# Attention sums loaded by head and multiplied by stored reciprocals, in the second stage of a two-layer graph network kernel

## What is computed

```python
# layer 0: masked attention with 8 heads of 16, then a feed-forward block
qkv = layer_norm(x, g1, be1) @ w_qkv
scores = einsum('nhd,mhd->hnm', q, k) * 16 ** -0.5      # masked by adj
out = einsum('hnm,mhd->nhd', softmax(scores), v).reshape(n, 128)
x = x + out @ w_proj + b_proj
ff = gelu(layer_norm(x, g2, be2) @ w1 + b1) @ w2 + b2
x = x + ff
# layer 1: attention whose score belongs to the row alone, projection, residual, layer norm
```

## Time and profile before

| | us |
|---|---|
| median of 3 runs | 1278.1 |
| lowest and highest run | 1275.76, 1278.79 |
| the profiled execution, its own time | 1278.86 |
| its span from first to last instruction | 1276.8 |
| PE busy | 1178.1 (92%) |
| DVE busy | 1138.7 (89%) |
| ACT busy | 1052.6 (82%) |
| POOL busy | 982.9 (77%) |

### The profile page before, as it was taken

How to read it: one execution, slowest core, us unless ns; L and a number is a source line. 1 busy time by engine, 2 the same in 40 slices (tenths; PEclk the granted TensorE clock), 3 DMA queues, 4 the chain that set the end, 5 groups by cost and what they waited for, 6 DMA issues and landing times. The chain is left out here.

```text
span 1276.8 us, 31455 instructions
## 1 busy us (share of the span) xinstructions
PE 1178.1 (92%) x11639; PEld 332.7 (26%) x11639; DVE 1138.7 (89%) x1616; ACT 1052.6 (82%) x1194; POOL 982.9 (77%) x1028
## 2 busy tenths in 40 slices
PE   5888889999999999999999899999999998999976
PEld 2222222111111111111111111111111126775433
DVE  5989889999999999999999899999999994656756
ACT  4978889999999999999999899999999992441000
POOL 5867768999999989999998788888888872544222
PEclk8989899999999999999999999999999998999988
DMA  4332324754554455555445545555455457405870
GB/s 175 91 117 75 84 87 129 209 157 134 165 151 134 133 167 160 155 150 162 138 133 163 147 143 158 154 153 145 133 167 149 134 154 292 180 20 236 328 301 28
DMA packets 52672, 194.40 MB, mean 152 GB/s; under 512 B 6497, under 2 KB 20641, under 8 KB 42273
## 3 DMA queue, kind: packets, MB, share of 16 engines
q1 hardware_dynamic: 38944, 156.65, 34.5%
q0 software_dynamic: 9216, 33.56, 12.9%
q10 hardware_dynamic: 4352, 2.10, 0.6%
HBM read 114.69 MB, written 44.04 MB: 124 GB/s over the span
## 5 line engine op out<-in xcount | busy, mean ns | idle before, releaser
L1394 DVE SCALAR_TENSOR_TENSOR probs<-m,ps 128x512 f32<-128x512 bf16 (+1 forms) x1024 | 926.6, 950 | 30.9 <-PE ps L1586 14.8
L1291 ACT ACTIVATE probs<-probs 128x1536 f32<-128x1536 f32 x512 | 848.5, 1658 | 0.9
L1188 POOL TENSOR_TENSOR probs<-probs,m 128x512 f32<-128x512 f32 x512 | 634.7, 1270 | 118.9 <-ACT probs L1285 107.9
L1601 PE MATMUL ps<-probs,v_sb 128*17 128x512 f32 x4096 | 543.5, 603 | 0.0
L1586 PE MATMUL ps<-kq 32*128 32x512 bf16 x6144 | 429.3, 382 | 61.6 <-DVE probs L1394 33.8
L1285 ACT ACTIVATE probs<-ps 128x512 f32<-128x512 f32 x512 | 392.1, 766 | 33.3 <-PE ps L1586 32.1
L1586 PEld LDWEIGHTS ps<-kq 32*128 32x128 bf16 x6144 | 117.0, 93 | 580.0 <-ACT probs L1285 429.8
L1181 POOL TENSOR_SCALAR m<-adj_in 128x512 bf16<-128x512 int32 x256 | 192.9, 754 | 0.2
L1601 PEld LDWEIGHTS ps<-probs,v_sb 128*17 128x17 f32 x4096 | 68.2, 95 | 219.8 <-issue 208.3
L453 ACT ACTIVATE probs<-ps 128x512 f32<-128x512 f32 x8 | 4.8, 597 | 86.1 <-PE ps L798 84.1
L376 POOL TENSOR_TENSOR v_sb<-v_sb,cols 128x4 f32<-128x4 f32 (+1 forms) x9 | 8.8, 975 | 74.3 <-DVE v_sb L649 74.3
(11 more groups left out here) (140 smaller groups left out, 652.0 us busy)
## 6 DMA issues: line engine op xcount, KB each, us to landing
adj_in<-in_adj_t SPq DMA_DIRECT2D x64, 1024.0 KB, 5.7
mask_t<-m SPq DMA_DIRECT2D x64, 512.0 KB, 2.9
counts<-m POOLq DMA_DIRECT2D x64, 512.0 KB, 4.6
kq<-mask_t SPq DMA_DIRECT2D x16, 2048.0 KB, 9.7
counts_t<-counts SPq DMA_DIRECT2D x8, 512.0 KB, 7.4
attn_t<-acc_sb SPq DMA_DIRECT2D x16, 256.0 KB, 6.7
adj_in<-attn_t SPq DMA_DIRECT2D x8, 512.0 KB, 3.9
v_sb<-counts_t SPq DMA_DIRECT2D x8, 512.0 KB, 7.0
```

What stands on the lines that cost most here:

```text
L1188: nc.gpsimd.tensor_tensor(pr, pr, m01[:, (k // 2) % MRING, :], ALU.mult).then_inc(postmasked, 1)
L1291: nc.scalar.activation(pr, pr, ACT.Exp, scale=UNIT).then_inc(exped, 1)
L1394: nc.vector.scalar_tensor_tensor(out=pr, in0=m.to_broadcast([P, n, CH]), scalar=1.0, in1=ps[:, b:b + n, :], op0=ALU.subtract, op1=ALU.add)\
L1601: last = nc.tensor.matmul(ps[RT * hh:RT * hh + VW, 6 + g, :], v_sb[:, t, h * VW:(h + 1) * VW], probs[:, k % SLOTS, hh // 2, (hh % 2) * CH: ...
```

## The change

Layout and order of the block stage change; what is computed stays.

- `load_sums` no longer loads the stored sums as they lie. It fetches only the 16 rows of each head, packed, so that row 16·head + d holds dimension d of that head: two transfers of 64 rows of 2 KB for the tile's first half, `outs[..][:, 0, :]`. A third one fetches the reciprocals from a new DRAM tensor `inverse_t`, each head's row of 512 repeated 16 times, into `outs[..][:, 1, :]`. With x these are four transfers a chunk in place of two.
- The reciprocals are made one chunk at a time during the attention: SP fetches the 17th rows of the chunk just stored in eight transfers (`load_head_sums`, 16x32 each) into a 128x32 tile, DVE inverts it (`invert`, called in `masks` at step 24 of the next chunk), SP stores it (`store_inverse`). For the last chunk SP does so in the block stage, with DVE's `invert` at `i == 0`.
- `normalise_att` is one 128x512 multiplication from SBUF to `attT`. `turn_acc`, `turn_att` and `turned_att` are gone, with PSUM banks 3 to 5 used by `turn_h2` alone.
- `project(i+1)` stands ahead of `ff1(i)`; `project(0)` between the third last and second last `products` of the attention.
- `x1` has two tiles, so `first_sum(c)` waits for the readers of chunk c-2.

The core of the diff:

```diff
         def load_sums(sp, c):
             if c >= 2:
-                sp.wait_ge(acc_turned, c - 1)
+                sp.wait_ge(attT_made, c - 1)
                 sp.wait_ge(xb_made, c - 1)
-            sp.dma_start(acc[c % 2][:, :, :], a_dram[c, :, :, :]).then_inc(acc_in[c % 2], 16)
+            for g in range(2):
+                rows_of = a_dram[c, :, g, :].rearrange("(h r) n -> h r n", r=RT)
+                sp.dma_start(outs[c % 2][g * HG * HD:(g + 1) * HG * HD, 0, :], rows_of[:, 0:HD, :])\
+                    .then_inc(acc_in[c % 2], 16)
+            sp.dma_start(outs[c % 2][:, 1, :], inv_dram[c].rearrange("h (a n) -> h a n", a=1).to_broadcast([H, HD, CH]))\
+                .then_inc(acc_in[c % 2], 16)
...
+        def load_head_sums(sp, c):
+            sp.wait_ge(acc_stored, 32 * (c + 1))
+            if c > 0:
+                sp.wait_ge(inverse_stored, 16 * c)
+            for g in range(2):
+                rows_of = a_dram[c % NC, :, g, :].rearrange("(h r) (s n) -> h r s n", r=RT, s=HD)
+                for hh in range(HG):
+                    at = (g * HG + hh) * HD
+                    sp.dma_start(head_sums[at:at + HD, :], rows_of[hh, HD, :, :]).then_inc(sums_in, 16)
+
+        def store_inverse(sp, c):
+            sp.wait_ge(inverted, c + 1)
+            sp.dma_start(inv_dram[c % NC].rearrange("h (s n) -> (h s) n", s=HD), head_sums[:, :])\
+                .then_inc(inverse_stored, 16)
+
+        def invert(dve, c):
+            dve.wait_ge(sums_in, 16 * H * (c + 1))
+            nc.vector.reciprocal(head_sums[:, :], head_sums[:, :]).then_inc(inverted, 1)
...
             load_sums(sp, 2)
             load_edges(sp, 1)
+            load_head_sums(sp, NC * R - 1)
             for n in range(2, ERING):
                 load_sums(sp, n + 1)
                 load_edges(sp, n)
+            store_inverse(sp, NC * R - 1)
...
             def normalise_att(c):
...
+                dve.wait_ge(acc_in[c % 2], LOADED * (c // 2 + 1))
                 if c >= 1:
...
+                    dve.wait_ge(projected, c)
+                nc.vector.tensor_tensor(attT, outs[c % 2][:, 0, :], outs[c % 2][:, 1, :], ALU.mult)\
+                    .then_inc(attT_made, 1)
...
             products(TLS * R - 4)
-            turn_acc(0)
             products(TLS * R - 3)
+            project(0)
             products(TLS * R - 2)
-            turn_att(0)
             products(TLS * R - 1)
-            project(0)
...
-            turn_acc(1)
             turn_h2(0)
             for i in range(NC):
-                ff1(i, (0, 1))
-                if i + 1 < NC:
-                    turn_att(i + 1)
-                ff1(i, (2, 3))
                 if i + 1 < NC:
                     project(i + 1)
+                ff1(i, (0, 1, 2, 3))
                 if i >= 1:
                     turn_x2(i - 1)
                 ff2(i)
-                if i + 2 < NC:
-                    turn_acc(i + 2)
...
+                if G >= per_chunk and G % per_chunk == 2:
+                    load_head_sums(sp, G // per_chunk - 1)
+                if G >= per_chunk and G % per_chunk == 4:
+                    store_inverse(sp, G // per_chunk - 1)
...
             def masks(k, begin):
+                if k >= begin + 2 * NT and k % (2 * NT) == 24:
+                    invert(dve, k // (2 * NT) - 1)
```

More of the change, by code:

```diff
@@ L383, in tail_scalar @@
             nc.scalar.activation(small[:, 7, 0:1], cols[:, 9:10], ACT.Gelu_apprx_tanh).then_inc(warmed, 1)
-            def turned_att(c):
-                act.wait_ge(att_turned, c + 1)
-                if c >= 1:
-                    act.wait_ge(projected, c)
-                nc.scalar.activation(attT, ps[:, B_TURN, :], ACT.Copy).then_inc(attT_made, 1)
             def turned_h2(c):
@@ L503, in first_sum @@
                 dve.wait_ge(xb_made, c + 1)
[L504 to L507 removed]
+                if c >= 2:
+                    dve.wait_ge(x1b_made, c - 1)
+                    dve.wait_ge(h2_made, c - 1)
+                nc.vector.tensor_tensor(x1[c % 2], by_tile(proj_bank(c)), xb[c % 2], ALU.add).then_inc(x1_made, 1)
                 dve.wait_ge(x1_made, c + 1)
                 for s in range(SUB):
[L510 removed]
+                    last = nc.vector.bn_stats(bn2[:, s, :], x1[c % 2][:, s, :])
                 last.then_inc(bn2_made, 1)
@@ L525, in normalise_x1 @@
                 for s in range(SUB):
-                    last = nc.vector.tensor_scalar(h2[:, s, :], x1[:, s, :], mv2[:, s, 0:1],
+                    last = nc.vector.tensor_scalar(h2[:, s, :], x1[c % 2][:, s, :], mv2[:, s, 0:1],
                                                    rstd2[:, s:s + 1], ALU.subtract, ALU.mult)
@@ L576, in tail_vector @@
                     normalise_att(i + 2)
+                if i == 0:
+                    invert(dve, NC * R - 1)
                 if i >= 1:
@@ L682, in tail_tensor @@
             pe.wait_ge(tail_in, N_TAIL_IN)
-            def turn_acc(c):
-                pe.wait_ge(acc_in[c % 2], 32 * (c // 2) + 32)
-                if c >= 1:
-                    pe.wait_ge(att_made, c)
-                else:
-                    pe.wait_ge(opened, TLS * R)
-                    pe.wait_ge(premasked, 2 * TLS * R)
-                for g in range(2):
-                    for s in range(SUB):
-                        last = nc.tensor.transpose(ps[:, B_ACC + g, s * P:(s + 1) * P],
-                                                   acc[c % 2][:, g, s * P:(s + 1) * P], identf[:, :])
-                last.then_inc(acc_turned, 1)
-            def turn_att(c):
-                pe.wait_ge(att_made, c + 1)
-                if c >= 1:
-                    pe.wait_ge(h2T_made, c)
-                for s in range(SUB):
-                    last = nc.tensor.transpose(ps[:, B_TURN, s * P:(s + 1) * P],
-                                               att[:, s * H:(s + 1) * H, :].rearrange("p h d -> p (h d)"),
-                                               identf[:, :])
-                last.then_inc(att_turned, 1)
             def project(c):
@@ L710, in project @@
                     pe.wait_ge(x1_made, c)
+                else:
+                    pe.wait_ge(opened, TLS * R)
+                    pe.wait_ge(premasked, 2 * TLS * R)
                 if c == 1:
@@ L1068, in second @@
                 store_acc(NC - 1)
-                sp.wait_ge(acc_stored, 32 * NC)
+                load_head_sums(sp, NC - 1)
+                store_inverse(sp, NC - 1)
+                sp.wait_ge(inverse_stored, 16 * NC)
                 sp.wait_ge(tail_in, N_TAIL_IN)
@@ L1085, in second @@
                         store_acc(G // per_chunk - 1)
+                    if G >= GROUPS + per_chunk and G % per_chunk == 2:
+                        load_head_sums(sp, G // per_chunk - 1)
+                    if G >= GROUPS + per_chunk and G % per_chunk == 4:
+                        store_inverse(sp, G // per_chunk - 1)
             def tail(sp, R):
@@ L1469, in second @@
                     copy_acc(NC - 1, g)
+                invert(dve, NC - 1)
                 all_reach(dve, phase)
```

49 lines of the change are left out of this document (14 added, 35 removed).

## The result

**Slower: 1283.61 us in the median of 5 executions (1281.56 to 1283.73), against 1276.79 (1275.40 to 1278.79) for the kernel before beside it, ratio 1.0049 [1.0035, 1.0063].** In a second measurement (`e0_changed` below) the ratio was 1.0038 [1.0022, 1.0054]. Forecast was 1274.6 in a range up to 1281.5. The profiled execution took 1281.56 us with a span of 1279.6, to be read against 1278.86 and 1276.8 before. That profile of before lies 2 to 3.5 us over the medians of its later runs (1275.4 to 1276.8), so differences of spans are good to about 3 us; differences inside one stage are sharper. The two profiled executions are 2.70 us apart, the medians 6.82: the profile of before is above all five of its runs, that of after is the shortest of its five.

The account below looks back on a forecast made before the run. PE was taken to bound the block stage, a DVE chain just under it. Attention +0.1, start and turn 0 0, turns -0.5, -1.9, -1.2 sum to -3.5: 1278.86 to 1275.4, 1274.6 on the median, range 1269.5 to 1281.5.

Parts of the forecast that it names:

- Start: Start of the block stage: `first_sum(0)` some 0.3 us earlier, PE at half clock, `ff1(0)` at 1062.8, 0.5 later.
- last paragraph: Signs for right or wrong; a load of sums landing after its multiplication could start would be something not counted.
- Turns: Block stage: turn 1 10.7 us, turns 2 to 5 10.75, turn 6 9.9; gains 0.5, 1.9 and 1.2 us.
- second chain: Block stage turn: `first_sum` through normalisation to `turn_h2`, 4.52 us, lies just under PE's bound; some tenths idle before `turn_h2`.
- Turn 0: First turn of the block stage: `ff1(1)` at 1075.15 against 1075.16 before, balance with the start 0.
- Attention: Seven added reciprocals on DVE cost 0.1 us in all, bounds nothing and 2.5; small transfers taken as nothing.
- Rival (c): Attention: POOL holds the reciprocals, 1.2 us each over seven, 8.4 in all, giving 1283.0, slower; chance 0.15.
- Rival (b): Block stage: the multiplication comes behind POOL's L335, waits 1.2 us, turn about 11.2, total 1277.6; chance 0.18.
- Rival (a): Block stage: PE alone bounds the turn, 9.91 us in turns 2 to 5, 3.4 more won, 1271.2; chance 0.17.
- Second x1 tile: Block stage: gives nothing, since the wait of `first_sum` ended with PE, not POOL.
- ACT's copy: ACT loses the copy L389; no gain, since it was not the bound.
- last stage: The stage after the block stage shifts whole, with no change of its own.

Follow-up runs that it names:

- e0_changed: The changed kernel measured once more, nothing altered: 1281.34 us, 1.0038 of the kernel before.
- e11: The kernel before, with only its load of sums replaced by the three transfers of the changed kernel (wrong data): 1285.12 us, 1.0053 of the kernel before.
- e4: The changed kernel with each chunk's sums and factors loaded in one transfer of 128 rows of 4 KB (wrong data): 1272.11 us, 0.9967 of the kernel before.
- e12: The changed kernel with the same rows picked and repeated in another order, 16 as outermost count, five transfers a load set: 1272.90 us, 0.9976 of the kernel before.
- e3: The changed kernel with picks kept, but reciprocals loaded from 128 distinct rows instead of repeated ones (wrong factors): 1274.58 us, 0.9966 of the kernel before.
- e6: The changed kernel with reciprocals still repeated, but sums loaded as 128 rows as they lie, without picking: 1272.37 us, 0.9977 of the kernel before.
- e9: The changed kernel with loads packed DRAM to DRAM during the attention, and `hidden_low` moved behind the normalisation: 1272.99 us, 0.9964 of the kernel before.
- e1: The changed kernel with `project(0)` moved behind the last two products: 1279.40 us, 1.0036 of the kernel before.
- e5: The changed kernel with `project(0)` behind the last two products and, on POOL, `root(0)` and `x1_bias(0)` ahead of `input_bias(1)`: 1280.12 us, 1.0027 of the kernel before.
- e13: The changed kernel with 16-outermost loads, `project(0)` behind the last products, `root(0)` and `x1_bias(0)` ahead of `input_bias(1)`: 1270.89 us, 0.9970 of the kernel before.
- e7: The changed kernel with picks and repeats made DRAM to DRAM during the attention, then one plain 512 KB load: 1270.93 us, 0.9948 of the kernel before.

## Why the prediction was wrong

**The step that failed: the loads of sums were not costed.** The step *Start* says "`normalise_att(0)` and `project(0)` leave the way of the last products earlier, so `first_sum(0)` starts right behind the second copy, some 0.3 before 1055.81". It took the new transfers to land like those of before (1050.1 and 1052.2), though the working names the other new DMAs and what each may delay. They landed at 1053.0 and 1061.4, and the start was 5.16 late, 6.16 counted from the end of the attention. The same omission made the turns from 1078.49 and 1101.35 last 12.08 and 13.30, 1.30 and 2.52 above 10.78: 3.8 of the 4.0 by which turns 1 to 5 missed; in the first of these two turns 0.73 of the 1.30 is the multiplication meeting POOL, which it does only because it is late. `e11` puts this on the loads alone, `e4` and `e12` take it away and leave the forecast's side: 0.9967 and 0.9976, where 1274.6 to 1278.1 was 0.9973. That agreement is closer than its parts (see the sum below) and in part luck. The last paragraph named "a load of sums landing after its multiplication could start" as something not counted. It was named and left without a price.

In the transfers the cause is the outermost count. Measured: counts of 4 and 8 give 228 GB/s, a count of 16 on the same rows 388. The Trainium skill ("DMA: Bandwidth & Descriptors", sections "Why a DMA increments its semaphore by 16 and not by 1" and "Rules for kernel authors") says that the slowest dimension of more than one element sets how many of the 16 engines a transfer runs on, and that for hardware-driven queues they are the lowest-numbered ones. The trace agrees with the number: 4 and 8 late steps for the transfers with counts of 4 and 8, and a DMA share of 0.24 to 0.25 at 90 to 99 GB/s while the last 4 steps of a mask load are outstanding. By that rule picks would lie on engines 0 to 3 and repeats on 0 to 7, on top of each other. The records do not number the engines, but that every mask load waits for just 4 late steps fits it.

One link is not shown: why the other engines slowed down too. The mean share stayed at 1.00 while the rate halved, so packets took longer in general. Those of 16 KB (the mask load's) that started from 1052 to 1056 took 0.61 us in the median before and in `e12`, 1.09 in the changed kernel and 1.10 in `e3`, but 0.62 in `e6`. So it comes with the picks, and its cause is open; the order in which `e12` reads the rows may have a part in it.

**Turns: right in size, partly wrong in reason.** Forecast 10.75, measured 10.78; last 9.9, measured 9.71. Timeline of PE over one turn of the changed kernel:

```profile
1125.43 3.79 PE L731 MATMUL ps<-q_shift,tail_words 128*128 128x512 f32 x8
1129.06 0.60 PE L723 MATMUL ps<-identf,probs 128*128 128x128 f32 x4
1130.00 3.84 PE L740 MATMUL ps<-tail_words,probs 128*128 128x128 f32 x32 [0.34 <-ACT probs L425]
1133.67 0.60 PE L713 MATMUL ps<-identf,q_shift 128*128 128x128 f32 x4
1134.11 1.00 PE L748 MATMUL ps<-tail_words,probs 128*128 128x65 f32 x8
1135.22 1.16 PE L704 MATMUL ps<-tail_words,q_shift 128*128 128x128 f32 x8
1136.21 3.79 PE L731 MATMUL ps<-q_shift,tail_words 128*128 128x512 f32 x8
```

`ff2` starts 4.57 after `ff1` (forecast 4.7), idle 0.34 for gelu. But `turn_h2` (L713) follows `ff2` without the "some tenths" of waiting: DVE's normalisation had ended at 1133.53, ahead of `ff2`. And `project` (L704) has a gap of about 0.1 behind `second_sum` and the multiplication. The "second chain" by way of `hidden_low` was just not binding; `e9`, which took `hidden_low` out of it, changed no turn. The bound is gelu ahead of `ff2`, then `ff2`, `second_sum`, multiplication, `project`. Of the 1.31 us taken from PE's turn 0.44 arrive in it. Waiting is the smaller part of the rest. PE is busy for 10.33 us of this turn, not for 9.91:

```profile
1125.43:1136.21 10.78, 10.33 (x66) 7.64 (x65) 6.66 (x21) 4.74 (x8) 6.04 (x6) 1.00 0.25 80
```

The pieces that stay take longer in the new order than the distances of the earlier trace rows: `ff1` 3.63 against 3.54, `turn_x2` 0.60 against 0.44, as PE then waits and nothing overlaps its end, `ff2` 3.67 against 3.57, `project` 0.99 against 0.89. The forecast had 0.6 us idle ahead of `ff2` and some tenths ahead of `turn_h2` instead; its 10.75 is right in part by luck.

**Turn 0: under-forecast.** Forecast -0.5, measured -1.83 (11.00), and 11.26 in `e12`. "PE ran at half clock here ... I keep the half clock" was the term: from `ff1(0)` to the end of `ff2` it takes 10.0 in the forecast (1062.8 to 1075.15, less 2.34), and 8.46 in the profile (1067.49 to 1075.95), since the clock came back during `ff1(0)` (granted 0.50 until 1067.9, 1.00 from then on), which took 4.01 against 3.79.

**Attention: right, as far as it can be read.** The view of L276 in the changed kernel:

```profile
L276 DVE RECIPROCAL head_sums<-head_sums x8: 343/345/353, 253.3 to 1081.9; 128x32 f32<-128x32 f32 x8
```

None of the eight was held by POOL. The 0.1 us itself can't be read off, since the end of the attention differs by up to 3 us from profile to profile. Rival (c) had the right side and the wrong reason: it stood on a hold of 1.1 us a piece. Of its chance of 0.15, 0.13 was all that was given to slower.

**Rival (b): order right.** Where the sums were there in time, the multiplication came ahead of POOL's `x2_bias`, 0.68 us; POOL's instruction paid instead, from 1.28 to 1.65, as the contention for two inputs in SBUF weighed in the prediction would have it:

```profile
1134.48 0.68 DVE L506 TENSOR_TENSOR q_shift<-adj_in 128x512 f32<-128x512 f32 x1
...
1134.64 1.65 POOL L364 TENSOR_TENSOR probs<-probs,tail_words 128x512 f32<-128x512 f32 x1 [2.26 <-DVE probs L544]
```

**Rival (a)**, a turn of 9.9, was wrong: PE itself needs 10.33, and the waits for gelu and `second_sum` come on top. **Second x1 tile, ACT's copy, last stage**: nothing gained or lost there. From `ff1(7)` to the end of the span is 134.4 us before and 133.7 after.

**The sum without the loads.** In `e12` `ff1(7)` starts at 1136.06, 6.3 before 1142.37, where -3.5 was forecast: start -1.15, turn 0 -1.57, turns 1 to 5 -2.2, turn 6 -1.4. In `e12` the attention itself ends 1.16 earlier than in the profile of before (1050.22 against 1051.38), which no step of the forecast is about. Without it the start is unchanged (+0.5 forecast), turn 0 gives 1.57 (0.5 forecast), and the sum is -5.15 against -3.6. The median of `e12` lies only 0.24% (about 3 us) under that of before. Part of the gap is the profile of before, 2 to 3.5 us over its medians; how much is not settled.

## What to carry to other kernels

When a change swaps one plain transfer for several with another pattern, write down for each its outermost count and bytes, and give it a price before anything that waits for it; then ask what stands behind it in the same queue, since here 2 MB mask loads that nobody touched took 18.3 us instead of 9.9. Where rows have to be picked or repeated, put a count of 16 outermost, or do it from DRAM to DRAM where there is time. A full DMA share beside half the GB/s is the sign to look for, and a wait that is taken away (`e1`, `e5`) may only show the next one for the same late data.

## What was unexpected in the hardware

- **Two mild forms, one bad sum.** Picks without repeats (`e3`, 280 GB/s) and repeats without picks (`e6`, 395 GB/s) were both no slower than before, 0.9966 (0.9994 by medians) and 0.9977; together they gave 230 GB/s and 1.0038. They are mild because in the turns no load of sums is late with either one (10.78 throughout), while both together cost 3.8 us there. At the start both cost: counted from the end of the attention `ff1(0)` comes 3.0 us later in `e3` than in `e4`, 1.8 later in `e6`, and 6.3 later in the changed kernel.
- **A blocked issue.** SP's issue of a mask load behind the new transfers took 2.89 us (L282 above), and the five of the stage 1.22 to 6.40, against 0.32 to 1.36 before. In `e12`, behind five transfers instead of four, the first took 0.50 and none over 1.54:

```profile
1050.14 0.50 SPq L283 DMA_DIRECT2D kq<-mask_t  x1
```

- **The clock can take an early start back.** `ff1(0)` of `e13` began 1.14 us before that of `e12` (1060.04 against 1061.18), but the clock came back to the 2.4 GHz level at the same time (1062.22 and 1062.15), so `ff1(0)` took 4.87 us instead of 4.27. It took 5.14 at 1062.38 in `e5` (back at 1065.11), and 4.01 at 1067.49 in the changed kernel (back at 1067.93). An early start need not lose: in `e9` it came at 1060.39 and took 4.06 (back at 1060.94). When the clock comes back differs from kernel to kernel, after 4.3 to 6.2 us in which PE stood idle, and no run here was made to find out why.
- **Left open.** In the last stage DVE waits 9 to 11 us for a store of the output in nearly every kernel, and a few executions of some were about 8 us shorter (1263.16 in `e7`). This was not studied.
